# Four-layer transformer: barriers, adapter loads and weight turning in another order at the stage seams

## What is computed

```python
for layer in range(4):
    xn = _layernorm(x)
    x = x + attn[layer](xn) + ffn[layer](xn)
```

```python
def _lora_linear(x, w, a, b):
    base = jnp.einsum('bsd,od->bso', x, w)
    low = jnp.einsum('bsr,or->bso', jnp.einsum('bsd,rd->bsr', x, a), b)
    return base + low * SCALING
```

## Time and profile before

| what | us |
|---|---|
| median of 3 runs | 2671.44 |
| lowest, highest | 2666.34, 2685.25 |
| the profiled execution's own time | 2670.21 |
| its span in the trace | 2668.4 |
| PE busy | 2470.2 (93%) |
| DVE busy | 1672.2 (63%) |
| ACT busy | 1030.8 (39%) |
| POOL busy | 937.3 (35%) |

### The profile page before, as it was taken

One profiled execution on the slowest core, in us unless ns is written; L12 is line 12 of the kernel. 1 busy time (PEld: TensorE's weight loads), 2 busy tenths in 40 slices (PEclk: granted clock), 3 DMA queues, 4 the chain that ended last, 5 costly groups with the idle time before them and its releaser, 6 DMA issues. The chain is left out here.

```text
span 2668.4 us, 40740 instructions
## 1 busy us (share of the span) xinstructions
PE 2470.2 (93%) x14448; PEld 1973.1 (74%) x14448; DVE 1672.2 (63%) x2382; ACT 1030.8 (39%) x2030; POOL 937.3 (35%) x581
## 2 busy tenths in 40 slices
PE   6999999699969889899999979999999999999897
PEld 4777767478846568788888868888888887888565
DVE  5886566464577676444544457878787786443574
ACT  3332155243236533213333345455445443323452
POOL 3342200234630124214444445555445544430000
PEclk9999999899979999999999989999999999999899
DMA  2232344773532022224444332322222222322420
GB/s 85 57 109 75 79 88 56 40 43 52 62 83 64 22 36 46 38 67 144 141 146 147 119 102 86 94 86 79 62 82 82 64 44 40 52 44 44 101 44 32
DMA packets 477242, 195.95 MB, mean 73 GB/s; under 512 B 351476, under 2 KB 430716, under 8 KB 477114
## 3 DMA queue, kind: packets, MB, share of 16 engines
q1 hardware_dynamic: 476856, 193.73, 32.6%
q10 hardware_dynamic: 258, 0.49, 0.1%
HBM read 129.43 MB, written 44.04 MB: 65 GB/s over the span
## 5 line engine op out<-in xcount | busy, mean ns | idle before, releaser
L596 PE MATMUL banks<-xn_hi,w_hi 128*128 128x512 f32 x1264 | 497.6, 394 | 11.4 <-ACT sgf L1139 8.6
L596 PE MATMUL banks<-xn_lo,w_hi 128*128 128x512 f32 x1264 | 493.9, 391 | 0.0
L596 PE MATMUL banks<-xn_hi,w_lo 128*128 128x512 f32 x1264 | 493.6, 391 | 0.0
L596 PEld LDWEIGHTS banks<-xn_hi,w_hi 128*128 128x128 f32 x1264 | 238.7, 189 | 62.8 <-DVE w_lo L584 9.4
L596 PEld LDWEIGHTS banks<-xn_hi,w_lo 128*128 128x128 f32 x1264 | 238.4, 189 | 49.9
L596 PEld LDWEIGHTS banks<-xn_lo,w_hi 128*128 128x128 f32 x1264 | 238.7, 189 | 48.7
L584 DVE TENSOR_TENSOR w_lo<-tw,w_hi 128x512 fp32r<-128x512 f32 (+2 forms) x144 | 128.4, 898 | 210.5 <-ACT w_hi L576 209.6
L3035 POOL TENSOR_TENSOR qk_raw<-qk_raw,rms 128x1024 f32<-128x1024 f32 x64 | 158.4, 2476 | 271.9 <-DMA qk_raw<-qk_scratch 260.4
L1251 POOL TENSOR_TENSOR h_lo<-sgf,h_hi 128x512 fp32r<-128x512 f32 (+1 forms) x94 | 126.4, 1348 | 321.5 <-ACT h_hi L1142 321.5
L2626 POOL TENSOR_TENSOR ssq<-ssq,sq 128x512 f32<-128x512 f32 x128 | 165.1, 1290 | 183.2 <-ACT sq L2597 183.2
L2614 DVE TENSOR_SCALAR raw<-banks,cols 128x512 f32<-128x512 f32 x128 | 103.7, 810 | 180.4 <-ACT sq L2597 180.4
(11 more groups left out here) (293 smaller groups left out, 5845.5 us busy)
## 6 DMA issues: line engine op xcount, KB each, us to landing
qk_scratch<-raw SPq DMA_DIRECT2D x64, 512.0 KB, 3.0
qk_raw<-qk_scratch SPq DMA_DIRECT2D x64, 512.0 KB, 3.8
nat<-in_L_ffn_w SPq DMA_DIRECT2D x48, 256.0 KB
head_scratch<-stage SPq DMA_DIRECT2D x16, 512.0 KB, 3.2
st_qs<-st_hi SPq DMA_DIRECT2D x64, 128.0 KB, 2.6
nat<-in_L_attn_Wq SPq DMA_DIRECT2D x32, 256.0 KB
nat<-in_L_attn_Wk SPq DMA_DIRECT2D x32, 256.0 KB
nat<-in_L_attn_Wv SPq DMA_DIRECT2D x32, 256.0 KB
```

The costliest lines, as they stand in the source:

```text
L596: mm = nc.tensor.matmul(to[half][:, :], w[0:n, j, k * P:(k + 1) * P], r, start=first and k == 0 and x == 0, stop=last and k == len(rows) - ...
```

## The change

1. **Barriers** of attention in layers 0, 1 and 3 (`att0`, `att1`, `att3`): on ACT and DVE they move ahead of the opening of W_o. PE and POOL keep theirs at the end of attention.
2. **Adapter loads** on SP: B1 and B3 are loaded and spread, both, ahead of the feed-forward loads of layer 1 (before, B1's load stood there, its spread and B3's load behind the first six loads of `up1`, B3's spread at the end of `up1`). A1/A3 follow the first six loads of `down1`. B2 and A2 are loaded and spread after layer 1's attention loads, ahead of those of W_o.
3. **Adapter splitting** on POOL: two operations instead of one after each tile of `up1` and `up2`; the seven operations for B2 move from the end of `down1` to the end of layer 1's attention, ahead of the barrier `att1`.
4. **Norm**: in `dve_up_first` the turning of chunks 4 and 5 moves behind the norm (chunk 4) and behind the next `dve_gated` (chunk 5); the low part of chunk 6 moves behind the last `dve_gated`. This code runs in layers 1, 2 and 3.
5. **`down2` on PE**: the adapter matmuls stand three chunks ahead instead of four.

```diff
             def at_end(left):
-                for k in {2: [0, 1], 0: [2, 3]}.get(left, []):
+                for k in {2: [0, 1], 0: [2]}.get(left, []):
                     pe_chunk_delta(pe, s.next, k)
...
             dve_gated(dve, s, 0)
-            dve_turn(dve, s, 4, 0, ALL)
             dve_squares(dve, s.norm, 1)
-            dve_turn(dve, s, 5, 1, ALL)
             dve_inverse(dve, s.norm, 1)
             dve_scale_x(dve, s.norm, 1)
             dve_low_x(dve, s.norm, 1)
+            dve_turn(dve, s, 4, 0, ALL)
...
             dve_gated(dve, s, 0)
+            dve_turn(dve, s, 5, 1, ALL)
...
             dve_turn(dve, s, 7, 3, ALL)
-            dve_lo(dve, s, 6, 2, ALL)
...
             dve_gated(dve, s, 1)
+            dve_lo(dve, s, 6, 2, ALL)
...
-                    n = ft - 2 * first
-                    if n < adapters[0].ops:
-                        pool_adapter(pool, adapters[0], [n])
-                    elif len(adapters) > 1:
-                        pool_adapter(pool, adapters[1], [n - adapters[0].ops])
+                    n = 2 * (ft - 2 * first)
+                    for adapter, at_ in zip(adapters, (0, adapters[0].ops)):
+                        pool_adapter(pool, adapter, range(max(n - at_, 0), min(n + 2 - at_, adapter.ops)))
...
-            proj_order(s, ahead, work, opening, LEAD_TURN if s.adapters else LEAD, seam_pe(pe, s))
+            proj_order(s, ahead, work, opening, seam=seam_pe(pe, s))
...
             sp_proj(sp, wo0, True)
+            sp_proj(sp, wo0)
             sp_adapter_load(sp, adapters[0])
-            sp_proj(sp, wo0)
+            sp_adapter_load(sp, adapters[1])
+            sp_adapter_spread(sp, adapters[0])
+            sp_adapter_spread(sp, adapters[1])
             sp_up(sp, up1, True)
-            sp_adapter_spread(sp, adapters[0])
-            sp_adapter_load(sp, adapters[1])
             sp_up(sp, up1)
-            sp_adapter_spread(sp, adapters[1])
             sp_proj(sp, down1, True)
-            sp_proj(sp, down1, adapters=adapters)
+            sp_adapter_load(sp, adapters[2])
+            sp_adapter_spread(sp, adapters[2])
+            sp_proj(sp, down1)
...
             sp_att(sp, att1)
+            for adapter in adapters[3:5]:
+                sp_adapter_load(sp, adapter)
+                sp_adapter_spread(sp, adapter)
             sp_proj(sp, wo1, True)
...
             act_att(act, att1)
+            barrier(act, "att1")
             act_proj(act, wo1, True)
-            barrier(act, "att1")
...
             dve_att(dve, att1)
+            barrier(dve, "att1")
             dve_proj(dve, wo1, True)
-            barrier(dve, "att1")
...
-            pool_adapter(pool, adapters[1], range(up1.nf - 2 - adapters[0].ops, adapters[1].ops))
             pool_adapter(pool, adapters[2])
-            pool_adapter(pool, adapters[3])
...
             pool_att(pool, att1)
+            pool_adapter(pool, adapters[3])
             barrier(pool, "att1")
```

More of the change, by code:

```diff
@@ L1375, in proj_order, with sp_proj @@
                 seam(0)
-        def sp_proj(sp, s, opening=False, adapters=None):
+        def sp_proj(sp, s, opening=False):
             def load(i, j, c):
@@ L1381, in load @@
                     sp.dma_start(dst(j), src).then_inc(loaded[j].sem, 16)
-            def store(i, j, c):
-                if adapters and i == 1:
-                    sp_adapter_load(sp, adapters[2])
-                if adapters and i == 2:
-                    sp_adapter_spread(sp, adapters[2])
-                if adapters and i == s.n // 2:
-                    sp_adapter_load(sp, adapters[3])
-                if adapters and i == s.n - 4:
-                    sp_adapter_spread(sp, adapters[3])
-                    sp_adapter_load(sp, adapters[4])
-                if adapters and i == s.n - 3:
-                    sp_adapter_spread(sp, adapters[4])
-            proj_order(s, load, store, opening, LEAD_LOAD)
+            proj_order(s, load, lambda i, j, c: None, opening, LEAD_LOAD)
         def pe_chunk_delta(pe, s, i):
@@ L3082, in pool_adapter @@
             v, to = lora_f[s.buf][0:LORA_ROWS, 0:width], s.to[0:LORA_ROWS, :]
-            for n in ops or range(s.ops):
+            for n in range(s.ops) if ops is None else ops:
                 if n == 0:
@@ L3313, in _ @@
             act_att(act, att0)
+            barrier(act, "att0")
             act_proj(act, wo0, True)
-            barrier(act, "att0")
             act_wo(act, wo0, norms[1], up1)
@@ L3349, in _ @@
             act_att(act, att3)
+            barrier(act, "att3")
             act_proj(act, wo3, True)
-            barrier(act, "att3")
             act_wo(act, wo3)
@@ L3367, in _ @@
             dve_att(dve, att0)
+            barrier(dve, "att0")
             dve_proj(dve, wo0, True)
-            barrier(dve, "att0")
             dve_wo(dve, wo0, norms[1], up1)
@@ L3397, in _ @@
             dve_att(dve, att3)
+            barrier(dve, "att3")
             dve_proj(dve, wo3, True)
-            barrier(dve, "att3")
             dve_wo(dve, wo3)
```

## The result

| | before | with the change |
|---|---|---|
| median, us | 2669.84 (20 runs) | 2683.53 (20 runs) |
| lowest, highest | 2658.70, 2685.25 | 2677.12, 2702.67 |
| ratio | | 1.0051, 95% interval 1.0035 to 1.0066 |
| span of the profiled execution | 2668.4 | 2676.4 |

The change makes the kernel 0.5% slower, 13.7 us by the medians; the forecast was +17.7 us. The two profiled executions lie only 8.0 us apart. Of the 5.7 us between these two figures, 3.5 lie in a stretch that the change doesn't touch (layer 2's attention, 670.9 us in the profile before and 667.4 after); experiment 5 shows how much that stretch scatters.

What follows compares the result with a forecast made beforehand. PE, busy 93% of the span, was taken as the bound. On the profiled 2670.2 us, +24.5 + 9.4 - 3.5 - 6.0 - 5.9 - 0.8 = +17.7 gave 2687.9, say 2688 us; range 2677 to 2701, own terms 2681 to 2697.

Steps and rivals of the forecast that it cites:

- first seam: Layer 0 into 1: W_gate's load waits in SP's queue behind B3 and both spreads, delaying DVE's turning and PE: +24.5 us.
- seam of layer 1: Barrier opens 1 us later behind POOL's B2 operations, then PE waits 8.36 us for all four turnings: +9.4 us.
- seam of layer 3: Without adapters, W_o's turnings follow the earlier barrier and PE needs only chunk 0's low part to start: -3.5 us.
- POOL's split in `down2`: Layer 2's feed-forward: two POOL operations a tile remove PE's 4.06 us wait and half-clock loss of 2 us: -6.0 us.
- turning in `down2`: Layer 2's feed-forward: a lead of three chunks removes PE's 4.43 us wait for chunk 2's turning, plus clock: -5.9 us.
- norm: Layers 1 to 3: chunk 4's turning no longer stands ahead of the three sums: -0.8 us in all.
- rival A: SP's queue at the first seam: the two B loads overlap, +8 instead of +24.5, total 2671 us; chance 10%.
- rival B: First seam: B3 takes its whole latency again, landing 26.2 us after B1; +32 there, total 2696 us; chance 13%.
- Rival D: Layer 1's seam: PE does not wait for W_o's turnings, about +2 instead of +9.4, total 2680 us; chance 8%.
- rival C: First chunks of down2: new waits at each tile give back the 11.9 us gained, total 2700 us; chance 14%.
- there is 0.1 us to gain: Norm in layer 1: sums began 1.24 us after ACT's squares, the first needs 2.17 us of squares, so 0.1 us to gain.
- The cost feared in the other direction: Behind the norm: slots of chunks 8 and 9 become free some 16 us later; norm bound of 3 us of loss.

Runs made afterwards that it cites:

- experiment 5: Changed kernel with one cause at layer 1's seam undone: barrier att1 back (2680.59 us), B2 back in layer 1's second projection (2677.98), or PE's wait for turnings dropped (2679.47).
- e1_sp0: Kernel before with only SP's new order at the first seam (B1, B3 and both spreads ahead of layer 1's feed-forward loads): 2692.91 us, ratio 1.0094.
- e12_oldnorm: Changed kernel with the old order in the norm's second half put back: 2688.72 us, ratio 1.0078 to the kernel before.
- e3_down2: Kernel before with two of POOL's A2 operations after each tile of up2, and down2's adapter matmuls three chunks ahead: 2660.17 us, ratio 0.9959.
- e4_lead: Kernel before with only down2's adapter matmuls moved to three chunks ahead: 2664.75 us, ratio 0.9978.
- e2_norm: Kernel before with only the new order of the norm's second half: 2667.48 us, ratio 0.9993.
- experiment 2: The norm's new order alone on the kernel before (2667.48 us, ratio 0.9993), and undone on the changed kernel (2688.72 us, ratio 1.0078).

## Why the prediction was right, and where it was off

The forecast was 2688 us, +17.7; measured were 2683.5, +13.7 (9.4 to 17.7 by the interval of the ratio). Term by term:

| term | forecast | measured, and by what |
|---|---|---|
| first seam | +24.5 | +26.2, end of attention to end of W_o; +25 alone (`e1_sp0`) |
| seam of layer 1 | +9.4 | +9.2 at PE's start, 16.93 against 7.75; +9.1 to +10.4 at the norm's second scaling, 70.0 in `e12_oldnorm` against 59.6 to 60.9 in the five kernels with the old norm and the old seam |
| seam of layer 3 | -3.5 | -3 to -4 |
| POOL's split in `down2` | -6.0 | -5 by the ratios, -6.5 by the profiles, `e3_down2` less `e4_lead` |
| turning in `down2` | -5.9 | -5.9, `e4_lead` |
| norm | -0.8 | about -8 between the scalings; with what comes behind -4.5 (`e2_norm`) to -10.4 (`e12_oldnorm`) |
| sum | +17.7 | about +12, with the norm at -8 |

- *Queue.* B3's issue took 17.58 us of the 22.63 (forecast 17.45), so that rival A (both loads side by side) is out. B3 landed 19 us after B1 (forecast 18.4, rival B 26.2). The spread of B3 went out a little later than thought, W_gate at 529.03 instead of 526.9, and it was turned 8.0 us on instead of 7.7. Rival B would have made the loss 32 us. The Trainium skill ("DMA: Bandwidth & Descriptors", section on queues, rings and completion order) has each DMA engine take the descriptors of SP's row in ring order; the 17.58 us agree with it once more.
- *Layer 1.* POOL's seven operations were the last thing ahead of the barrier, and PE began only behind the fourth turning (966.44, start 966.58). Rival D is out. The undoings show what the prediction only implied: the two causes are one path, and either one removed gives 7.7 us at PE's start.
- *`down2`.* Both waits are gone and no others came there; rival C is out. The new wait of 1.1 us on L480 is one of `up2`, and belongs to the norm (experiment 2).
- *Norm: the step that failed.* The prediction wrote "there is 0.1 us to gain" and looked only at when the sums start. It had three sums at 3.33 us in view, and three of them take 2.29 us undisturbed. The 1.04 us between the two was the collision with POOL. The 0.1 us was real, and it decided who came first; the shorter wait of PE and, in some kernels, its clock came on top. The cost feared in the other direction, slots freed 16 us later, did not show in layer 1; in layer 2 the new order costs 1.2 to 1.6 us there, 1.1 of them a wait for a turned chunk.
- *How much of it is luck.* The large terms, the two seams and `down2`, came from the mechanisms that the prediction gave, and the norm was off by some 4 to 10 us. That this term's miss and the 4.0 us between the medians are alike says little: the interval of the measured difference is 8 us wide, and layer 2's attention alone scatters by 15 us from profile to profile.
- *Two sums in the prediction don't come out.* PE's waits at the places of the change are 51.1 us, not 41 (the 10.5 us of the barrier stand there twice, for layers 0 and 3). And where it takes its terms at their bounds, the lower end of 2681 has all of them, the upper end of 2697 doesn't: with all upper bounds it is 2706. Neither enters the forecast of 2688.

In SP's list B1 and B3 stand behind the loads of W_o, and those SP has done only when attention ends. The diff names where a step is written; the timeline of its queue says when it happens.

## What to carry to other kernels

An issue is placed by the time at which its queue reaches it: look for the idle stretch in that queue's timeline, and put long element-wise loads there (moving two such loads turned this change from 0.5% slower into 1.1% faster). Before a barrier is moved ahead of work, list what each engine does last before it, and what the first instruction behind it asks for; work that ran beside the slowest engine otherwise stands in a row behind it. And where a row's total is more than its count times the usual duration, look for the other engine that ran at that moment, before taking the start alone for the gain. Last, follow a gain past the place of the edit: of the 7.7 us that an undoing gave at PE's start in layer 1, 4.4 to 4.6 were left one norm further on.

## What the runs showed of the hardware

- A 0.06 us difference in start decides over 1.06 us of a DVE operation (0.69 or 1.75 us) when POOL reads SBUF at the same time, and the winner loses nothing.
- The same 3415 matmuls of layer 2's attention took from 665 to 680 us in fourteen profiled executions; the mean granted clock was 0.97 in the four longest and 0.98 in the others.
- Eight small matmuls of PE took 1.05 us behind a wait of 3.74 us in one kernel and 1.69 behind one of 1.78 in another: the wait just before does not by itself tell which clock PE has.
- The element-wise load held the next issue on SP for 17.6 us at the seam. Inside attention, B3 was issued at 331.69, and the unit's loads behind it, issued from 357.84, still took 11.2 us: there it landed after 38.3 us, and it cost attention nothing.
